# A graph attention and expert kernel: the subtraction of one from the adjacency moved from DVE to POOL

## The reference, cut to what matters

```
h = layernorm(x)
Wh = h @ W
e = leaky_relu(Wh @ a[:F] + (Wh @ a[F:]).T, 0.2)
att = softmax(where(adj > 0, e, -9e15), axis=1)
h_prime = att @ Wh
x = x + gru(h_prime, h)          # gates from h_prime @ w_ih.T and h @ w_hh.T
# then: top 2 of 16 experts per token, silu(x2 @ w1) * (x2 @ w2) @ w3, weighted sum, plus x
```

## Time and profile before

| | |
|---|---|
| median of 3 runs | 1316.3 us (1313.3 to 1320.53) |
| profiled execution, own time | 1322.15 us |
| its span, first to last instruction | 1320.4 us |
| PE, DVE, ACT, POOL busy | 1195.2, 1019.8, 779.5, 355.0 us |
| mean granted clock of PE | 0.945 of full speed |
| subtractions of one, all on DVE | 128 in 51.1 us |
| masks on DVE | 128 in 158.8 us |
| transfers of the adjacency | 128, each 4.6 us from issue to landing (median) |

### The profile page before, as it was taken

One profiled execution on the slowest core, in us unless ns is written; L12 is line 12 of the kernel. 1 busy time (PEld: TensorE's weight loads), 2 busy tenths in 40 slices (PEclk: granted clock), 3 DMA queues, 4 the chain that ended last, 5 costly groups with the idle time before them and its releaser, 6 DMA issues.

```text
span 1320.4 us, 25406 instructions
## 1 busy us (share of the span) xinstructions
PE 1195.2 (91%) x7317; PEld 1035.0 (78%) x7319; DVE 1019.8 (77%) x2445; ACT 779.5 (59%) x1141; POOL 355.0 (27%) x351
## 2 busy tenths in 40 slices
PE   5675999999999999999999997259999999999995
PEld 4445888888888898989898986148888888888884
DVE  5336788888888888888888875688888888888883
ACT  3227666666666666666666652006666666666662
POOL 1322111010101011111111100015656555555553
PEclk9767999999999999999999998659999999999998
DMA  6204424242424242424243400042354364345430
GB/s 200 56 1 64 63 55 77 57 77 57 77 57 77 57 77 56 77 57 77 57 77 57 77 25 21 13 150 53 52 137 96 55 187 135 91 93 146 93 48 8
DMA packets 61630, 98.60 MB, mean 75 GB/s; under 512 B 9472, under 2 KB 36096, under 8 KB 61536
## 3 DMA queue, kind: packets, MB, share of 16 engines
q0 software_dynamic: 33600, 52.49, 25.3%
q1 hardware_dynamic: 27936, 44.93, 10.5%
HBM read 213.18 MB, written 18.81 MB: 176 GB/s over the span
## 4 chain that ended last, share of the span: by engine, by line
PE 61%; DVE 16%; DMA 9%; ACT 6%; issue 4%; POOL 3%; POOLq 0%; DVEq 0%; SPq 0%; ACTq 0%
PE bank L1221 11%; PE bank L1012 11%; DMA out<-ysc,cidx 9%; PE bank L1130 8%; PE bank L1235 7%; PE bank L1107 5%; PE bank L1106 5%; PE bank L1108 5%; PE bank L1133 4%; DVE pc L751 3%; ACT E L551 2%; PE bank L1040 2%; ACT pc L482 1%; POOL rs L434 1%; DVE scr L788 1%
## 5 line engine op out<-in xcount | busy, mean ns | idle before, releaser
L1106 PE MATMUL bank<-V,pc 128*128 128x258 f32 x1024 | 311.2, 304 | 3.5 <-DVE pc L751 3.5
L1107 PE MATMUL bank<-V,pc 128*128 128x258 f32 x1024 | 291.6, 285 | 0.0
L1108 PE MATMUL bank<-V,pc 128*128 128x258 f32 x1024 | 289.3, 283 | 0.0
L482 ACT ACTIVATE pc<-bank 128x512 fp32r<-128x512 f32 x256 | 152.1, 595 | 173.0 <-PE bank L1012 169.6
L1221 PE MATMUL bank<-wup,xT 128*128 128x512 f32 x948 | 239.4, 401 | 0.9 <-DVE xT L959 0.9
L751 DVE TENSOR_TENSOR pc<-bank,pc 128x512 fp32r<-128x512 f32 x256 | 176.4, 689 | 64.4 <-ACT pc L482 59.9
L1221 PEld LDWEIGHTS bank<-wup,xT 128*128 128x128 f32 x948 | 174.4, 191 | 35.1 <-DVE xT L959 1.3
L1106 PEld LDWEIGHTS bank<-V,pc 128*128 128x128 f32 x1024 | 194.0, 189 | 4.6 <-DVE pc L751 4.6
L1108 PEld LDWEIGHTS bank<-V,pc 128*128 128x128 f32 x1024 | 196.1, 192 | 0.0
L1107 PEld LDWEIGHTS bank<-V,pc 128*128 128x128 f32 x1024 | 196.1, 191 | 0.0
L954 DVE TENSOR_TENSOR wup<-wexp,wup 128x1024 fp32r<-128x1024 f32 x158 | 185.8, 1217 | 2.3 <-ACT wup L482 1.4
(11 more groups left out here) (155 smaller groups left out, 1645.4 us busy)
## 6 DMA issues: line engine op xcount, KB each, us to landing
wexp<-in_L_ffn_w SPq DMA_DIRECT2D x237, 512.0 KB
adjb<-in_adj POOLq DMA_DIRECT2D x128, 256.0 KB, 4.6
token_rows<-xrow SPq DMA_DIRECT2D x32, 130.0 KB, 2.2
E<-in_x SPq DMA_DIRECT2D x8, 512.0 KB, 5.3
xin<-in_x SPq DMA_DIRECT2D x32, 128.0 KB, 2.7
out<-xin SPq DMA_DIRECT2D x32, 128.0 KB, 1.7
xg<-token_rows,gidx POOLq DMA_INDIRECT x79, 3.6
out<-ysc,cidx POOLq DMA_INDIRECT x79, 3.8
```

Of the source, the lines that this page charges most:

```text
L482: act_copy = lambda o, i: nc.scalar.activation(o, i, ACT.Copy)
L1106: mm(acc[:, 0:VW], hi, V[:, j, 0, :], start=j == 0, stop=False)
L1107: mm(acc[:, 0:VW], hi, V[:, j, 1, :], start=False, stop=False)
L1108: ins = mm(acc[:, 0:VW], lo, V[:, j, 0, :], start=False, stop=j == T - 1)
```

## The change

POOL makes the subtraction in place of DVE. Four subtractions of tile 0 stand before POOL's first loads of tile 1, and the four of tile i+1 at the head of POOL's body i. The operation, its operands and the semaphore that it raises are the same. DVE's calls go away, and its masks wait for `s_am` as before.

```diff
+            def less_one(n, q):
+                pool.wait_ge(s_adj[q], n * 16 + 16)
+                nc.gpsimd.tensor_scalar(adjb[:, q, :], adjb[:, q, :], 1.0, None, ALU.subtract).then_inc(s_am, 1)
+
+            for q in range(Q):
+                less_one(0, q)
             for q in range(Q):
                 pool.wait_ge(s_ms, q + 1)
                 load_adj(1, q)
 
             def body(i):
+                if i + 1 < T:
+                    for q in range(Q):
+                        less_one(i + 1, q)
                 if i + 2 < T:
                     for q in range(Q):
                         pool.wait_ge(s_ms, (i + 1) * Q + q + 1)
...
-            def less_one(n, q):
-                dve.wait_ge(s_adj[q], n * 16 + 16)
-                V_.tensor_scalar(adjb[:, q, :], adjb[:, q, :], 1.0, None, ALU.subtract).then_inc(s_am, 1)
-
...
             dve.wait_ge(s_const, CONSTS)
-            less_one(0, 0)
-            less_one(0, 1)
             mask_logits(0, 0)
-            less_one(0, 2)
             mask_logits(0, 1)
-            less_one(0, 3)
             mask_logits(0, 2)
             mask_logits(0, 3)
...
             def body(i):
                 ahead = i + 1 < T
-                if ahead:
-                    less_one(i + 1, 0)
-                    less_one(i + 1, 1)
                 if live(i, 1):
                     combine(i - 1)
                     remake_xn(i - 1)
                 if ahead:
                     mask_logits(i + 1, 0)
-                    less_one(i + 1, 2)
                     mask_logits(i + 1, 1)
-                    less_one(i + 1, 3)
                     mask_logits(i + 1, 2)
```

## The result

| | median of the runs | against before |
|---|---|---|
| before | 1318.41 us (1313.3 to 1328.33, 4 runs) | |
| changed | 1397.38 us (1393.87 to 1398.95, 4 runs) | 1.0586, 95% interval 1.0518 to 1.0654 |

The change costs about 77 us (5.86% of 1318). The forecast was +22 us; the time lies above the range, which ended at 1390. The side and the two places of the loss were right, their sizes were not. The ratios further down are each to runs of the kernel before that were made beside that version, with medians of 1317.2 to 1321.2 us.

What follows compares the result with a forecast made beforehand. The prediction took a closed chain around each attention tile through ACT, DVE, POOL and PE as the bound, with nothing overlapping at the start. Steady tiles 14.8 plus start 7.3 gave +22 us, 1338 us; range 1318 to 1390.

Steps and rivals of the forecast that it cites:

- price X of one subtraction (part 2): Time of one 1024-element subtraction on POOL, taken as 1.25 us, between bounds of 0.95 and 2.35.
- exclusion (part 3): Attention masks on DVE and POOL's subtractions shut each other out; four subtractions and three masks run end to end, 4X + 3 x 1.09 us.
- 4X - 4.47: Growth of each steady attention tile in us, X being one POOL subtraction; 0.53 us at X = 1.25.
- +14.8 us: Loss in the steady attention tiles: 0.53 us in each of 28 tiles, from tile 4 on.
- no exclusion: Rival: POOL's one-input subtractions leave the masks alone and run beside them; only the start pays about +4, 1320 us; 7%.
- Slow POOL: Rival: one POOL subtraction takes above 1.4 us; at 1.66 a tile grows by 2.17 us, +70, 1386 us; 31%.
- closed chain (part 1 and the first section): Around each attention tile, row maximum, ACT, DVE, `pow`, `xrow` and PE wait in turn; a later row maximum lengthens the tile.
- room of 0.53 us: ACT's one gap in a steady tile, ahead of its copy at 516.87; a row maximum delay up to it costs nothing.
- DVE's relief: Taking 128 subtractions, 51.1 us busy, 1.68 us per tile, off DVE was costed at a gain of nothing.
- The place behind the `pow` (part 4): POOL subtracts for tile i+1 only after the previous body's `pow`, in the masks' window; loss begins at X = 1.12.
- The start (part 5): Tile 0's subtractions wait behind POOL's last two-input subtraction, so its row maximum comes 7.3 us later, all of it showing.
- 4X + 2.26: Delay of tile 0's row maximum in us, X being one POOL subtraction; 7.3 us at X = 1.25.

Runs made afterwards that it cites:

- bench: The kernel before with a trial ahead of it: POOL runs several instruction forms alone, then DVE runs beside them; scalar subtraction 2.77 to 2.79 us, two-input 1.89.
- beside_alone: The kernel before without any adjacency subtraction, POOL instead subtracting one from an unused tile at the changed kernel's place, no mask waiting for it; 1336.23 us.
- pool_512: The changed kernel with each POOL subtraction cut to 512 of its 1024 columns; 1327.87 us.
- pool_256: The changed kernel with each POOL subtraction cut to 256 of its 1024 columns; 1325.04 us.
- no_less: The kernel before with no subtraction on either engine; the mask adds 1 at an edge, 0 elsewhere, and the row maximum removes the shift; 1314.9 us.
- start_pool: The changed kernel with only tile 0's four subtractions on POOL, all others on DVE as before; 1328.34 us.
- pool_tt: The changed kernel with POOL's subtraction of a scalar replaced by subtraction of a tile of ones; 1430.42 us.

## Why the prediction was wrong, point by point

Two steps failed: the price of one subtraction on POOL, and the exclusion.

**The price X of one subtraction (part 2) failed.** The two-input subtraction of 2.35 us was taken as the upper bound, without a reason; behind it stands that one input can't cost more than two. The scalar form costs 2.77 us, above the bound, and in bench it is dearer than the two-input form also with POOL alone (2.79 against 1.89). This is the term that was mis-sized, 1.25 against 2.77, and it is what the total turns on.

**The exclusion (part 3) failed for this form.** Both collided masks of the earlier trace rows had met an instruction with two inputs. Beside the scalar form DVE is held 1 us of 2.8, and in the order of the changed kernel POOL is not held up by the masks: four take 11.01 us, 2.75 each from start to start, where one alone takes 2.79 (bench). So the series of 4X and three masks is not there. What is there is 4X and then the fourth mask: 11.01 + 1.63 us from the `pow` to the row maximum. Less the 9.42 of before and the room of 0.86, a tile grows by 4X - 8.65, which for X = 2.75 is 2.35 us, 2.36 measured. The prediction's 4X - 4.47 would give 6.5 us for that X. The assumption that POOL waits for a mask, for which it had no row, holds where the mask runs first (beside_alone, pool_512).

**The two errors pulled apart.** With X = 1.25 as assumed, no tile would have waited, since 4X - 8.65 is below zero up to X = 2.16, and by pool_512 and pool_256 only `xrow` and the start would be paid: the +14.8 us had the wrong reason. X was too small and the exclusion too dear, and the two errors work against each other. The rival "no exclusion", with 7%, had the mechanism of the start, 4X - 1.0: with X = 2.75 that gives the 10.0 measured. "Slow POOL", with 31%, had the nearest time, 1386, by luck: its X of 1.66 is 1.1 us too small, and the exclusion that is not there makes up for it, with 2.17 us per tile against 2.36.

**The closed chain (part 1 and the first section) held.** Its room of 0.53 us was too small, the two traces give 0.86. ACT had a second gap, too small to be bracketed: in the kernel before its first exponential ends at 512.54, and the copy behind it starts at 512.66, 1.31 us after the row maximum. In the changed kernel both gaps are gone.

```profile
512.66 0.60 ACT L482 ACTIVATE pc<-bank 128x512 fp32r<-128x512 f32 x1
```

```profile
516.35 0.59 ACT L491 ACTIVATE pc<-bank 128x512 fp32r<-128x512 f32 x1
```

The first line is of the kernel before, the second of the changed one, where it is the copy ahead of the last exponential. This copy starts 516.35 - 511.69 = 4.66 us after the row maximum, and before 516.87 - 511.35 = 5.52. That is the whole 0.86.

DVE's relief was worth nothing in the steady tile, which no_less shows by itself: 21.89 with none of it.

**The place behind the `pow` (part 4) held**, and it is why "a tile ahead" bought nothing. What was overlooked there is that the first subtraction starts in the same moment as `xrow`, right behind the same `pow`. PE waits for `xrow` 0.40 us per tile already, so this costs 0.72 us per tile by itself (beside_alone). In the changed kernel it is taken to be hidden behind the larger wait, as 4X - 8.65 leaves nothing for it. **The start (part 5)** was forecast at 7.3 us and came to 10.0, and start_pool shows it alone. Part 5 too had the exclusion in it: with X = 2.75 its 4X + 2.26 would be 13.3.

## What to carry to other kernels

An instruction that moves to POOL is priced by its own form. Here subtracting a scalar took 2.77 us, subtracting a tensor 1.89 and copying 1.04 for the same 1024 elements, and nothing but a trial of the form told that. Ask what is released in the same moment as the moved work, and what DVE does beside it: the time that POOL holds the port falls on the DVE instruction that meets it, if it is of a kind that is held, and a short one is held as long as a long one. And before work is moved off an engine, ask whether its time there is paid for, and whether the work is needed: here it was hidden, and leaving it out was the only version that gained.

## What the runs showed of the hardware

- POOL's subtraction of a scalar takes the same 2.77 to 2.79 us in bf16 and in f32, and 1.49 us for half the elements. The affine select of 128 elements had pointed to 1.0 to 1.7.
- A DVE instruction with two SBUF inputs is held at the head of POOL's scalar subtraction (1.05 us of 2.80), for all of a two-input one (1.89 of 1.89), and not at all by a memset (0.19 us, its usual time). One with one input and a scalar is held by the memset as well (1.01 us instead of 0.17). In pool_512 and pool_256 the hold on `xrow` went from 0.72 to 0.29 and 0.08 us.
- POOL in turn is held when it starts while a mask runs: its scalar subtraction takes 3.64 us instead of 2.77 in beside_alone and 2.49 instead of 1.49 in pool_512, its two-input one 3.11 instead of 2.10 to 2.18 in pool_tt. When it starts first it is not (2.77 us in the changed kernel, 2.79 alone). In pool_tt even the others take more than the 1.89 us of the trial, in which both inputs were one tile; why is open. Why the value part's two-input subtraction takes 2.35 us instead of 1.89 is open.
